# Two cross-attention layers on one core: the second batch's turned x and first context groups issued ahead of layer 1's value and output weights

## The chip, the cores and the metric

The kernel runs on 1 core of one Trainium2 chip. The metric is the device time of one execution in microseconds (us), the median of several runs.

## The reference

Eight batches (B = 8) with x of 512 x 256 and a context `ctx` of 1601 x 128, all float32, go through two cross-attention layers with the same context. Cut to what matters:

```python
# layer 0, for each batch: the softmax runs over the 512 rows of x (axis=1)
q = x @ Wq0 + bq0;  k = ctx @ Wk0 + bk0;  v = ctx @ Wv0 + bv0
w = softmax((q @ k.T) / 16, axis=query rows)
h = layernorm(w @ v + x) * gamma + beta
# layer 1: the softmax runs over the 1601 context rows
Q = h @ Wq1 + bq1;  K = ctx @ Wk1 + bk1;  V = ctx @ Wv1 + bv1
out = h + (softmax((Q @ K.T) / 16) @ V) @ Wo1 + bo1
```

## The kernel before

**Tiling.** The 1601 context rows are 13 tiles of at most 128 (`MT`), in 4 groups (`GROUPS`): three of four tiles (512 rows) and one of 65 rows. `ctxT` is the context turned, 128 x 1601; `xT` is x turned, two tiles of 128 x 512. The key and query weights are multiplied with each other once at the start (`make_w0`, `make_w1` item 0), so that the scores are taken straight from `ctxT` and a projected x. The value and output weights of layer 1 are multiplied with each other too, in `make_w1` item 1, which waits for `wv_loaded`.

**Order of the work.** Every engine follows an order that is written out by hand as a list of (step, batch, item): a head, a steady part repeated for four batches, and a tail. Engines meet only in semaphores. The steps that this text speaks of, with the line of each one's instruction:

- TensorE (PE). `project_q0(a)` (line 669) projects `xT` of batch a, and waits for `xT_loaded`. `project_bias0(a)` (676) turns a row sum `z0` into a row, `scores0(a, i)` (643 to 645, three matmuls) makes the layer-0 scores of context tile i, `weigh0(a, i)` (705) multiplies the context with the weights of tile i. `predict(0, h)` (643 to 645 again) makes the layer-0 result. Their order in the head around the change: scores0(0, 5), project_q0(1), scores0(0, 6), weigh0(0, 2), scores0(0, 7), weigh0(0, 3), (0, 4), (0, 5), scores0(0, 8), project_bias0(1).
- VectorE (DVE). `max0` (1086) takes scores out of PSUM and finds the least of each row of the negated ones; `recip0` (1093) is the reciprocal of a sum of exponentials; `q0_low` (1062) is one half of the split of the projected x; `sum_z0` (1076) makes `z0`; `ctxT_low` (1047) splits the turned context; `prepare_w1` item 0 (1228) adds `beta_row` and `bo_row`, item 2 (1241) makes `u1_gamma`, item 3 (1056) splits the value weights. In the order: max0(0, 5), ctxT_low(0, 3), recip0(0, 4), recip0(0, 5), q0_low(1), max0(0, 6), max0(0, 7), prepare_w1 item 0, recip0(0, 6), sum_z0(1), recip0(0, 7), max0(0, 8).
- ScalarE (ACT). `exp0` (919) and `norm0` (925) work on `p0`, the weights of one tile; `q0_high` (904), `ctx_split` (898) and `ctx_high` (890) round to fp32r; `copy_w1` (1017 to 1028) brings the prepared weights out of PSUM. In the order: exp0(0, 5), q0_high(1), norm0(0, 4), norm0(0, 5), ctx_split(0, 3), exp0(0, 6), ctx_split(1, 0), exp0(0, 7), ctx_split(1, 1), norm0(0, 6), norm0(0, 7), ctx_split(1, 2), ctx_high(1, 0), exp0(0, 8).
- GpSimd (POOL). `sum_weights(a, i)` (1284, 1287) adds `p0` of tile i to the running sum `wsum`, `weigh_u0(1)` (1318) multiplies x of batch 1 (the plain rows, `x_sb`, loaded by `load_x(1)`) with a row. In the order: sum_weights(0, 1), weigh_u0(1), sum_weights(0, 2), (0, 3), (0, 4), ctx_low(0, 3), sum_weights(0, 5), ...
- SyncE (SP) issues nearly all transfers, in the order of `pre0` and of the loop behind it. `load_xT(1)` waits for `qw0_ps` (project_q0(0) has read `xT_sb`), `load_ctxT(1, 0)` waits for the first `ctxT_low`; `load_ctx(1, 0)` waits for nothing.

**Rings.** `p0` has four slots for tiles 0 to 11 and a fifth for tile 12. `exp0(0, 6)` takes the slot of tile 2, and so waits for both its readers:

```python
if (held := before0(a, i)) is not None:
    back, last = held
    act.wait_ge(pv0_ps, MT * (a - back) + last + 1)
    act.wait_ge(wsum_done, summed(a - back, last))
```

and `weigh_u0(1)` begins with `pool.wait_ge(x_loaded[a % 2], 16 * (a // 2 + 1))`.

Of the kernel before, what the change touches and what calls it, by code (L numbers as in the profile page):

```python
# [300 lines left out]
def xattn_kernel(nc, x, xT, ctx, ctxT, wqT0, wkT0, wqT1, wkT1, wvT1, columns, wv0, bv0, gamma, beta, wo, bo, out):  # L301
    B, T, E = x.shape
    _, M, L = ctx.shape
    TB = T // P
    EC = E // P
    MT = -(-M // P)
    MPAD = M + M % 2
    GROUPS = -(-MT // TB)
# [35 lines left out]
    def rows(i):  # L344
        return min(P, M - i * P)

    def group(g):
        return range(TB * g, min(TB * g + TB, MT))

    def group_cols(g):  # L350
        return TB * g * P, min(M, TB * (g + 1) * P)
# [9 lines left out]
    with ExitStack() as stack:  # L361
# [196 lines left out]
        @blk.sync  # L558
        def _(sp):
            def load_x(c):  # L560
                if c >= 2:
                    sp.wait_ge(xbias_done, c - 1)
                sp.dma_start(x_sb[c % 2][:], x[bass.ds(c, 1)].rearrange("o (t p) e -> p (o t) e", p=P)
                             ).then_inc(x_loaded[c % 2], 16)

            def load_xT(c):

                if c >= 1:
                    sp.wait_ge(qw0_ps, c)
                sp.dma_start(xT_sb[:], xT[bass.ds(c, 1)].rearrange("o (c p) t -> p (o c) t", p=P)).then_inc(xT_loaded, 16)  # L570

            def load_ctxT(c, g):

                if c >= 1:
                    sp.wait_ge(ctxT_lo_done, GROUPS * (c - 1) + g + 1)
                lo, hi = group_cols(g)
                sp.dma_start(ctxT_sb[:, lo:hi], ctxT[bass.ds(c, 1), :, lo:hi].rearrange("o l m -> (o l) m")
                             ).then_inc(ctxT_loaded[g], 16)

            def load_ctx(c, g):  # L580

                if c >= 2:
                    sp.wait_ge(ctx_lo_done, GROUPS * (c - 2) + g + 1)
                    sp.wait_ge(pv0_ps, MT * (c - 2) + group(g)[-1] + 1)
                full = [i for i in group(g) if rows(i) == P]
                if full:
                    src = ctx[bass.ds(c, 1), full[0] * P:(full[-1] + 1) * P, :]
                    sp.dma_start(ctx_sb[c % 2][:, full[0]:full[-1] + 1, :], src.rearrange("o (i p) l -> p (o i) l", p=P)
                                 ).then_inc(ctx_loaded[c % 2][g], 16)
                else:  # L590
                    i = group(g)[0]
                    src = ctx[bass.ds(c, 1), i * P:M, :]
                    sp.dma_start(ctx_sb[c % 2][0:rows(i), i, :], src.rearrange("o p l -> (o p) l")).then_inc(ctx_loaded[c % 2][g], 16)

            def pre0():
                sp.dma_start(wqT[0], wqT0.rearrange("(h p) e -> p h e", p=P)).then_inc(w_loaded[0], 16)
                load_xT(0)
                load_ctxT(0, 0)
                load_x(0)
                load_ctx(0, 0)  # L600
                for g in range(1, GROUPS):
                    load_ctxT(0, g)
                    load_ctx(0, g)
                sp.dma_start(wqT[1], wqT1.rearrange("(h p) e -> p h e", p=P)).then_inc(w_loaded[1], 16)
                sp.dma_start(wkT[1], wkT1.rearrange("(h p) l -> p h l", p=P)).then_inc(w_loaded[1], 16)
                sp.dma_start(wv0_sb, wv0).then_inc(wv_loaded, 16)
                sp.dma_start(wvT, wvT1.rearrange("(h p) l -> p h l", p=P)).then_inc(wv_loaded, 16)
                sp.dma_start(wo_sb, wo.rearrange("(c p) d -> p c d", p=P)).then_inc(wv_loaded, 16)
                for row, v, landed in ((bv0_row[:], bv0, rows_loaded), (gamma_row[:], gamma, rows_loaded),
                                       (beta_row, beta, out_free[0]), (bo_row, bo, out_free[1])):  # L610
                    sp.dma_start(row, v.rearrange("(o e) -> o e", o=1).broadcast_to([P, E])).then_inc(landed, 16)
                load_x(1)

            def store(b):
                dst = out[bass.ds(b, 1)].rearrange("o (t p) e -> p (o t) e", p=P)
                for h in range(2):
                    sp.wait_ge(o_done, 2 * b + h + 1)
                    sp.dma_start(dst[:, 2 * h:2 * h + 2, :], y_res[:, 2 * h:2 * h + 2, :]
                                 ).then_inc(out_free[h], 16)

            pre0()
            for c in range(1, B + 3):
                if c < B:
                    load_xT(c)
                    for g in range(GROUPS):
                        load_ctx(c, g)
                        if g < GROUPS - 1:
                            load_ctxT(c, g)
                if c >= 3:
                    store(c - 3)  # L630
                if 2 <= c < B:
                    load_x(c)
                if c < B:
                    load_ctxT(c, GROUPS - 1)
            for h in range(2):
                sp.wait_ge(out_free[h], 16 * (B + 1))
# [3 lines left out]
        def _(pe):  # L640
# [22 lines left out]
            def project_q0(a, _):  # L663
                pe.wait_ge(xT_loaded, 16 * (a + 1))
                misc_free("project_q0", a)
                if a == 0:
                    pe.wait_ge(a0_done, 1)
                for c in range(EC):
                    mm = nc.tensor.matmul(ps_misc[:], a0_sb[:, c, :], xT_sb[:, c, :], start=(c == 0), stop=(c == EC - 1))  # L669
                mm.then_inc(qw0_ps, 1)  # L670

            def project_bias0(a, _):
                pe.wait_ge(z0_done, a + 1)
                misc_free("project_bias0", a)
                for t in range(TB):
                    mm = nc.tensor.transpose(ps_misc[:, t * P:(t + 1) * P], z0[:, t:t + 1].broadcast_to([P, P]), ident[:])
                mm.then_inc(cb_ps, 1)
# [698 lines left out]
```

## Time and profile before

| | us |
|---|---|
| median of 3 runs | 459.2 |
| lowest and highest run | 459.0 and 460.92 |
| the profiled execution, its own time | 460.37 |
| its span, first to last instruction | 458.4 |

In the profiled execution TensorE is busy for 430.9 us (94% of the span), VectorE 369.7 (81%), ScalarE 366.1 (80%), GpSimd 312.6 (68%). Some 2.0 us of the execution's time lie outside the span. The change touches the first 24 us of the kernel; times in the rows are counted from the start of the span.

### The profile page before, as it was taken

What the parts mean: (1) busy time and instruction counts of PE and PEld (TensorE: products, weight loads), DVE (VectorE), ACT (ScalarE), POOL (GpSimd) and SP (SyncE); (2) the same over time, 40 slices, a digit from 0 to 9 for tenths busy, and PEclk for the clock granted to TensorE, in tenths of its full rate; (3) what the DMA queues carried; (4) which work ended last, traced back from release to release, by engine and by line L of the source; (5) the groups of instructions that cost most, each with busy time, mean ns of one, the idle gap of its engine ahead of it and who ended that gap; (6) DMA issues with size and microseconds to landing.
All of it is one profiled execution on the core that took longest, in us unless ns stands there. A gap on an engine that the chain in (4) does not pass through costs nothing.

```text
span 458.4 us, 7304 instructions
## 1 busy us (share of the span) xinstructions
PE 430.9 (94%) x2192; PEld 340.9 (74%) x2192; DVE 369.7 (81%) x871; ACT 366.1 (80%) x776; POOL 312.6 (68%) x279
## 2 busy tenths in 40 slices
PE   7799799999999999999999999999999989897796
PEld 5555577788778877787788877787778876586696
DVE  3678887789778998799878998799788887586775
ACT  3877499989799878989799878988988788853473
POOL 1586489937996599847995599846995589813400
PEclk9999799999999999999999999999999999998999
DMA  8943012112132032302131032302200010000001
GB/s 273 287 140 93 19 54 72 48 46 74 48 98 65 1 117 73 94 0 76 45 115 48 1 117 74 93 1 68 54 1 1 0 46 2 1 1 23 24 1 46
DMA packets 31190, 28.00 MB, mean 61 GB/s; under 512 B 2856, under 2 KB 26032, under 8 KB 31152
## 3 DMA queue, kind: packets, MB, share of 16 engines
q1 hardware_dynamic: 30736, 27.41, 19.7%
q8 instruction: 17, 0.28, 0.3%
q10 hardware_dynamic: 416, 0.14, 0.1%
q14 instruction: 21, 0.17, 0.1%
HBM read 23.35 MB, written 4.19 MB: 60 GB/s over the span
## 4 chain that ended last, share of the span: by engine, by line
PE 73%; DVE 12%; ACT 6%; issue 3%; SPq 3%; DMA 2%; POOL 1%; DVEq 0%; ACTq 0%; POOLq 0%
PE ps_s L643 11%; PE ps_s L645 9%; PE ps_s L644 9%; PE ps_s L765 9%; PE ps_l L643 7%; PE ps_l L705 7%; PE ps_l L645 7%; PE ps_l L644 7%; ACT p L976 2%; DVE max L1170 2%; PE ps_l L669 2%; DMA xT_sb<-in_xT_dram 2%; DVE xhT_lo L1153 2%; DVE s_sb L1086 1%; DVE y_res L1213 1%
## 5 line engine op out<-in xcount | busy, mean ns | idle before, releaser
L1287 POOL TENSOR_TENSOR wsum<-wsum,p 128x512 f32<-128x512 f32 (+1 forms) x88 | 115.1, 1308 | 15.2 <-ACT p L925 7.5
L1294 POOL TENSOR_TENSOR p_lo<-p,p_hi 128x512 fp32r<-128x512 f32 (+1 forms) x49 | 63.8, 1303 | 44.9 <-ACT p_hi L933 44.7
L919 ACT ACTIVATE p<-s_sb,min 128x512 f32<-128x512 f32 (+1 forms) x104 | 75.0, 721 | 16.0 <-PE ps_l L705 9.5
L925 ACT ACTIVATE p<-p,r 128x512 f32<-128x512 f32 (+1 forms) x104 | 73.0, 720 | 7.0 <-DVE r L1093 6.9
L1086 DVE CUSTOM_DVE_ANT_0 s_sb<-ps_l,cb 128x512 f32<-128x512 f32 (+1 forms) x104 | 70.1, 686 | 10.2 <-PE ps_l L645 6.1
L1170 DVE TENSOR_REDUCE max<-ps_s 128x1 f32<-128x804 f32 x58 | 57.5, 993 | 16.4 <-PE ps_s L645 14.9
L1098 DVE TENSOR_TENSOR p1T_lo<-ps_s,p1T_hi 128x512 fp32r<-128x512 f32 (+1 forms) x91 | 59.8, 684 | 11.6 <-ACT p1T_hi L984 10.9
L984 ACT CAST p1T_hi<-ps_s 128x512 fp32r<-128x512 f32 (+1 forms) x91 | 51.2, 586 | 17.3 <-PE ps_s L765 9.8
L976 ACT ACTIVATE p<-ps_s,bias 128x1206 f32<-128x1206 f32 (+1 forms) x58 | 53.1, 920 | 3.8 <-DVE bias L1181 3.7
L705 PE MATMUL ps_l<-p,ctx_sb 128*128 128x512 f32 (+1 forms) x110 | 55.4, 596 | 0.0
L643 PE MATMUL ps_l<-qw_hi,ctxT_lo 128*128 128x512 f32 (+1 forms) x104 | 51.3, 493 | 1.2 <-DVE ctxT_lo L1047 0.8
L765 PEld LDWEIGHTS ps_s<-ident,p 128*128 128x128 f32 (+1 forms) x364 | 42.7, 140 | 10.4 <-issue 2.6
L765 PE MATMUL ps_s<-ident,p 128*128 128x128 f32 (+1 forms) x364 | 49.6, 273 | 0.4 <-ACT p L976 0.4
L1275 POOL TENSOR_TENSOR ctx_lo<-ctx_sb,ctx_hi 128x512 fp32r<-128x512 f32 (+1 forms) x32 | 34.4, 1079 | 16.9 <-ACT ctx_hi L898 16.9
L643 PE MATMUL ps_s<-ctxT_hi,qw_lo 128*128 128x402 f32 x116 | 42.1, 363 | 2.4 <-ACT p L976 1.6
L643 PE MATMUL ps_s<-p1T_hi,ctx_lo 128*128 128x512 f32 (+2 forms) x104 | 43.3, 416 | 0.6 <-DVE p1T_lo L1193 0.6
L644 PE MATMUL ps_l<-qw_lo,ctxT_hi 128*128 128x512 f32 (+1 forms) x104 | 41.5, 399 | 0.0
L645 PE MATMUL ps_l<-qw_hi,ctxT_hi 128*128 128x512 f32 (+1 forms) x104 | 41.5, 399 | 0.0
L645 PE MATMUL ps_s<-ctxT_hi,qw_hi 128*128 128x402 f32 x116 | 39.9, 344 | 0.0
L644 PE MATMUL ps_s<-ctxT_lo,qw_hi 128*128 128x402 f32 x116 | 39.8, 343 | 0.0
L644 PE MATMUL ps_s<-p1T_lo,ctx_hi 128*128 128x512 f32 (+2 forms) x104 | 39.7, 382 | 0.0
L645 PE MATMUL ps_s<-p1T_hi,ctx_hi 128*128 128x512 f32 (+2 forms) x104 | 39.5, 380 | 0.0
(161 smaller groups left out, 1039.7 us busy)
## 6 DMA issues: line engine op xcount, KB each, us to landing
ctxT_sb<-in_ctxT_dram SPq DMA_DIRECT2D x24, 256.0 KB, 2.7
ctx_sb<-in_ctx_dram SPq DMA_DIRECT2D x24, 256.0 KB, 3.2
xT_sb<-in_xT_dram SPq DMA_DIRECT2D x8, 512.0 KB, 3.8
x_sb<-in_x_dram SPq DMA_DIRECT2D x8, 512.0 KB, 4.1
out_dram<-y_res SPq DMA_DIRECT2D x16, 256.0 KB, 2.2
p<-in_wqT_dram SPq DMA_DIRECT2D x2, 256.0 KB, 4.0
ctxT_sb<-in_ctxT_dram SPq DMA_DIRECT2D x8, 32.5 KB, 1.8
ctx_sb<-in_ctx_dram SPq DMA_DIRECT2D x8, 32.5 KB
```

The source lines that it names most:

```text
L643: nc.tensor.matmul(ps, w_lo, m_hi, start=start, stop=False)
L644: nc.tensor.matmul(ps, w_hi, m_lo, start=False, stop=False)
L645: return nc.tensor.matmul(ps, w_hi, m_hi, start=False, stop=stop)
L705: mm = nc.tensor.matmul(ps_acc0[:], ctx_sb[a % 2][0:m, i, :], p0[0:m, ring0(i), :], start=first, stop=last)
L765: mm = nc.tensor.transpose(ps_turn[i % 3][0:m, t * P:(t + 1) * P], p1[:, t, i * P:i * P + m], ident[:])
L919: nc.scalar.activation(p0[0:m, ring0(i), :], s0_sb[0:m, (a + i) % 2, :], ACT.Exp, bias=min0[0:m, i:i + 1], scale=-1.0, accum_out=sum0[0:m, ...
L925: nc.scalar.activation(p0[0:m, ring0(i), :], p0[0:m, ring0(i), :], ACT.Copy, scale=r0[0:m, i:i + 1]).then_inc(norm0_done, 1)
L976: nc.scalar.activation(exps, scores, ACT.Exp, bias=bias1[:, t:t + 1], scale=1.0, accum_out=sum1[:, h, t:t + 1]).then_inc(exp1_done, 1)
L1086: nc.vector.tensor_tensor_reduce(out=s0_sb[0:m, (a + i) % 2, :], in0=ps_s0[0:m, (a + i) % 2, :], in1=cb[a % 2][0:m, :], scale=-SCALE, scal ...
L1170: nc.vector.tensor_reduce(max1[:, t, k:k + 1], s1_banks(b, t)[:, 2 * k:2 * k + 2, 0:CHUNK], AX_XY, ALU.max).then_inc(max1_done, 1)
L1287: nc.gpsimd.tensor_tensor(total, total, p0[0:m, ring0(i), :], ALU.add).then_inc(wsum_done, 1)
L1294: nc.gpsimd.tensor_tensor(p0_lo[0:m, h, :], p0[0:m, ring0(i), :], p0_hi[0:m, h, :].bitcast(F32), ALU.subtract).then_inc(p0_lo_done, 1)
```

## The change

In `pre0` of SyncE three transfers are issued right behind the query and key weights of layer 1: `load_xT(1)` (512 KB), `load_ctxT(1, 0)` (256 KB) and `load_ctx(1, 0)` (256 KB). The layer-0 value weights `wv0`, the layer-1 weights `wvT` and `wo`, four row vectors spread over the partitions (`bv0_row`, `gamma_row`, `beta_row`, `bo_row`) and `load_x(1)` follow them. The loop leaves the three out in its first turn. No other engine's program changes.

```diff
                 sp.dma_start(wkT[1], wkT1.rearrange("(h p) l -> p h l", p=P)).then_inc(w_loaded[1], 16)
+                load_xT(1)
+                load_ctxT(1, 0)
+                load_ctx(1, 0)
                 sp.dma_start(wv0_sb, wv0).then_inc(wv_loaded, 16)
                 sp.dma_start(wvT, wvT1.rearrange("(h p) l -> p h l", p=P)).then_inc(wv_loaded, 16)
                 sp.dma_start(wo_sb, wo.rearrange("(c p) d -> p c d", p=P)).then_inc(wv_loaded, 16)
...
             for c in range(1, B + 3):
+                if 1 < c < B:
+                    load_xT(c)
                 if c < B:
-                    load_xT(c)
                     for g in range(GROUPS):
-                        load_ctx(c, g)
-                        if g < GROUPS - 1:
-                            load_ctxT(c, g)
+                        if (c, g) != (1, 0):
+                            load_ctx(c, g)
+                            if g < GROUPS - 1:
+                                load_ctxT(c, g)
```

## Rows read from the trace of the kernel before

**Rows 1.** TensorE's timeline, 7 to 50 us: start, us, instructions, [idle before <-releaser].

```profile
7.86 1.96 PE L669 MATMUL ps_l<-xT_sb,a_sb 128*128 128x512 f32 x4
...
22.36 1.98 PE L669 MATMUL ps_l<-xT_sb,a_sb 128*128 128x512 f32 x4 [1.98 <-DMA xT_sb<-in_xT_dram]
...
30.55 0.65 PE L676 MATMUL ps_l<-ident,z 128*128 128x128 f32 x4 [0.68 <-DVE z L1076]
...
33.28 1.03 PE L855 MATMUL ps_s<-p 128*128 128x256 f32 x4
...
49.67 0.58 PE L643 MATMUL ps_l<-wv_hi,at_lo 128*128 128x256 f32 x1 [1.57 <-DVE xr L1126]
```

**Rows 2.** SyncE's timeline, 9 to 16 us: start, us to issue, transfer.

```profile
9.46 0.47 SPq L606 DMA_DIRECT2D p<-in_L_xattn_Wv_dram  x1
...
12.89 0.43 SPq L563 DMA_DIRECT2D x_sb<-in_x_dram  x1
13.37 0.51 SPq L570 DMA_DIRECT2D xT_sb<-in_xT_dram  x1
...
15.41 1.36 SPq L577 DMA_DIRECT2D ctxT_sb<-in_ctxT_dram  x1
```

**Rows 3.** The last three of these issues in the DMA view: size, us from issue to landing.

```profile
x_sb<-in_x_dram SPq DMA_DIRECT2D x1, 512.0 KB, 8.0
xT_sb<-in_xT_dram SPq DMA_DIRECT2D x1, 512.0 KB, 8.9
ctxT_sb<-in_ctxT_dram SPq DMA_DIRECT2D x1, 256.0 KB, 8.5
```

**Rows 4.** The chain that ended last, 40 to 50 us, in order of time.

```profile
40.93 0.24 PE ps_l L645
...
41.33 0.18 DVE s_sb L1086
```

**Rows 5.** GpSimd's timeline, 17 to 44 us.

```profile
20.97 2.34 POOL L1318 TENSOR_TENSOR xr<-x_sb,u_row 128x1024 f32<-128x1024 f32 x1 [2.13 <-DMA x_sb<-in_x_dram]
23.28 4.10 POOL L1287 TENSOR_TENSOR wsum<-wsum,p 128x512 f32<-128x512 f32 x3
...
36.78 6.95 POOL L1287 TENSOR_TENSOR wsum<-wsum,p 128x512 f32<-128x512 f32 x5 [2.64 <-ACT p L925]
```

**Rows 6.** ScalarE's timeline, 26 to 31 us.

```profile
26.50 0.72 ACT L919 ACTIVATE p<-s_sb,min 128x512 f32<-128x512 f32 x1
...
27.73 0.72 ACT L919 ACTIVATE p<-s_sb,min 128x512 f32<-128x512 f32 x1
...
29.41 0.72 ACT L925 ACTIVATE p<-p,r 128x512 f32<-128x512 f32 x1 [0.36 <-DVE r L1093]
30.60 0.72 ACT L925 ACTIVATE p<-p,r 128x512 f32<-128x512 f32 x1 [0.46 <-DVE r L1093]
```

**Rows 7.** VectorE's timeline, 21 to 43 us.

```profile
21.18 2.22 DVE L1047 TENSOR_TENSOR ctxT_lo<-ctxT_sb,ctxT_hi 128x65 fp32r<-128x65 f32 x1
...
29.30 1.20 DVE L1076 TENSOR_REDUCE z<-xr 128x4 f32<-128x1024 f32 x1
...
39.63 1.56 DVE L1241 SCALAR_TENSOR_TENSOR u_gamma<-p,gamma_row 128x256 f32<-128x256 f32 x1
41.33 0.69 DVE L1086 CUSTOM_DVE_ANT_0 s_sb<-ps_l,cb 128x512 f32<-128x512 f32 x1
...
41.95 0.65 DVE L1056 TENSOR_TENSOR wv_lo<-p,wv_hi 128x256 fp32r<-128x256 f32 x1
```

**Rows 8.** Busy us by stretch: PE, PEld, DVE, ACT, POOL, PEclk, DMA share, GB/s.

```profile
15.00:18.00 3.00, 3.00 (x13) 2.05 (x13) 1.51 (x5) 2.69 (x6) 0.74 (x2) 1.00 0.60 155
18.00:24.00 6.00, 4.02 (x14) 2.16 (x12) 4.12 (x11) 3.87 (x11) 3.87 (x3) 1.00 1.06 344
...
30.60:41.40 10.80, 10.80 (x48) 7.66 (x49) 7.85 (x23) 10.80 (x24) 7.59 (x7) 1.00 0.24 74
49.60:55.80 6.20, 6.13 (x18) 4.79 (x18) 5.93 (x20) 2.74 (x6) 3.08 (x4) 0.51 0.00 0
```

## The prediction

> **What bounds the kernel now.** I read TensorE's timeline first. It stands still for 1.98 us before project_q0(1), until the turned x of batch 1 has landed [rows 1], while ahead of that transfer on SyncE's queue lie weights and rows that nobody wants for another 5 to 10 us. That is what the change is about, and 1.98 us is the most that its direct effect can give. Behind it, in 30.6 to 41.4 us, TensorE and ScalarE are both busy without a gap [rows 8]. So both must get earlier for the end to get earlier. From 41.33 us the chain of waits runs on VectorE, started by the score matmul that ends at 41.17 [rows 4]. VectorE hands over at 49.67 us, when TensorE has waited 1.57 us for it at predict(0, 1) [rows 1]. After that TensorE is nearly always busy, and a shift of this point passes to the end one for one. The question is thus when VectorE's work of 41.33 us starts afterwards.
>
> **Part 1: the moved transfers.** Landings follow from issue and duration [rows 2, 3]: x(1) at 12.89 + 8.0 = 20.9, xT(1) at 13.37 + 8.9 = 22.3, ctxT(1, 0) at 15.41 + 8.5 = 23.9 us. GpSimd's start at 20.97 and TensorE's at 22.36 agree [rows 1, 5]. They land in the order of issue, and each waits some 8 us: the queue is backed up, so a place in it is what counts. xT(1), ctx(1, 0) and ctxT(1, 0), 1 MB, take from 20.93 to 23.9, 2.97 us.
> Afterwards xT(1) has ahead of it neither the 512 KB of value and output weights, nor four spread rows, nor x(1). That is 1.5 MB less, at the 344 GB/s of 18 to 24 us [rows 8] 4.6 us: it lands by 17.7 us, rather sooner, since the spread rows were slower than that. TensorE, which comes at 22.36 - 1.98 = 20.38 us, doesn't wait: minus 1.98 us there.
> The added wait: SyncE comes to load_xT(1) at 9.46 us [rows 2] and must wait until project_q0(0) has read the old xT, 7.86 + 1.96 = 9.8 us [rows 1]: some 0.4 us, with all later issues queued behind it. The wait for the first ctxT_low is over by then. The queue's backlog of several us covers the 0.4; if it were empty, the transfers behind would be 0.4 late. The three extra issues, 0.5 us each, lie under the same cover. The weights for make_w1 item 1 and the spread rows land ahead of x(1), so before 23.9 us; the first are wanted at 33.28 [rows 1], and prepare_w1 item 0, which wants rows, isn't reached before 25.1. The context groups behind the moved ones have the same bytes ahead as before.
>
> **Part 2: what becomes late.** x(1) now has 1 MB more ahead: 20.93 + 2.97 = 23.9 us. Bounds: at the 344 GB/s of 18 to 24 us [rows 8] 1 MB takes 3.05 us; if the three lie in a stretch like 15 to 18 us, 155 GB/s, 6.8 us. That slow stretch falls on the spread rows, which pass whole both times, so I take the near value, 2.97. Nothing of it is a gain: at best x(1) stays at 20.93.
> GpSimd already waits 2.13 us for x(1) [rows 5], and its order puts weigh_u0(1) before sum_weights(0, 2). It starts at 23.95, ends 2.31 later at 26.26, and the sum of tile 2 takes 1.27: 27.53 us. ScalarE's exp0(0, 6) takes over tile 2's slot and must wait for that sum. Now the sum is ready at 23.28 + 1.37 = 24.6 and exp0(0, 6) starts at 26.50 without waiting for it [rows 6]; afterwards it starts at 27.6, 1.1 us later than before, though its scores are 2 us earlier. The next, exp0(0, 7), follows the sum of tile 3, at 28.97 against 27.73: plus 1.24.
> ScalarE makes up its two idle pieces, 0.36 and 0.46 us [rows 6], because VectorE's reciprocals are no longer what it waits for. With one of the usual steps of 0.63 between, norm0(0, 6) comes at 30.3 and norm0(0, 7) at 30.9, against 30.60: plus 0.3 us. From there to 41.4 us ScalarE has no gap [rows 8], so exp0(0, 8), the reciprocals, norm0(0, 8) and copy_w1 items 1 to 3 are all 0.3 late.
>
> **Part 3: TensorE between.** It does scores0(0, 6) to (0, 8) and four weighings some 2 us earlier, and stands at project_bias0(1) from 27.6. sum_z0(1) is behind recip0(0, 6) on VectorE, which follows exp0(0, 6): 27.6 + 0.82 + 0.1 = 28.5, plus 1.2 for the reduction [rows 7]: 29.75 us against 30.50. So of 1.98 us TensorE keeps 0.75. It loses 0.4 of this again at weigh0(0, 8), whose norm0 is ScalarE's, and makes the score matmul of 41.17 us end at about 40.8.
>
> **Part 4: VectorE at 41.33.** It doesn't start there at 40.97, for u1_gamma (1241) comes before. That step needs copy_w1 item 1 (plus 0.3), and it took 1.56 us, from 39.63 to 41.19, though it is 128 x 256 [rows 7]. ctxT_low of 65 columns took 2.22 us, and ended as GpSimd's weigh_u0 did [rows 5, 7]: such a step waits until GpSimd's running instruction is over. GpSimd's five sums start with norm0(0, 8), 0.3 late, so the sum that lets u1_gamma go ends 0.3 late too: 41.5 us. VectorE goes on at 41.55 to 41.6 instead of 41.33, and the value split (1056), which also took 0.65 us between GpSimd's sums, is released 0.3 later. The sum is **plus 0.3 us** at 49.67 and at the end. Profiled execution: 460.37 + 0.3 = 460.7; it lies 1.2 above the median of the runs, so on the median's scale 459.2 + 0.3 = **459.5 us**.
> The least that this can be: if GpSimd's timing lets VectorE through and only TensorE decides, minus 0.36 (458.8). The most: weigh_u0 and the sums now run without pause until 36 us, and ctxT_low(1, 0) and the split of a1_gamma lie under them; each can wait up to 1.3 us. They have about 0.6 us of room before norm0(0, 9) and exp0(0, 11) wait for them. One more such hit gives plus 1.0 (460.2).
>
> **Two rules weighed.** The row shows a 65-column ctxT_low of 2.22 us beside GpSimd's 2.34 us multiplication [rows 5, 7]. The Trainium skill, "SBUF — State Buffer", section "Who interferes with whom", says that a VectorE instruction with two SBUF inputs and a GpSimd one that reads SBUF exclude each other for the whole instruction, and that PSUM-fed or one-input steps are free. The trace agrees; by this rule weigh_u0 from 23.95 lies on prepare_w1 item 0 instead of on ctxT_low(0, 3), and without the rule part 4 would come out at minus 0.3.
> The rows give 2.97 us for the moved 1 MB. The Trainium skill, "DMA: Bandwidth & Descriptors", section "Where 436 GB/s comes from", puts the fabric's ceiling at 435 GB/s, and HBM's at about 358. At 435 it would be an estimated 2.4 us and the sum minus 0.3; at 358 it would be 2.9. The trace's 344 GB/s stands near the second.
>
> **Rivals.** (a) *The full gain.* If exp0(0, 6) weren't held by x(1), ScalarE, TensorE and VectorE would all move by the 1.98 us: 457.2. ScalarE's shift is x(1)'s landing minus 23.6 us, so this needs x(1) by 21.6. For it: the slow stretch of 155 GB/s [rows 8] might be due to the order of the queue and vanish, and then x(1) lands up to 2 us sooner. Against it: the DMA engines are full in 18 to 24 us. Chance 0.18, cases between 457.0 and 458.6.
> (b) *x(1) later still* (the other side). It lands behind weights, rows and 1 MB; if the slow stretch gets longer, ScalarE, and with it VectorE, is late by landing minus 23.6. x(1) at 25.6 gives plus 2.0, 461.2; it is slower by over 0.5%, 2.3 us, from 25.9 us on. For it: GpSimd has no slack at all here. Against it: the same bytes. Chance 0.14.
> (c) *The clock.* TensorE's idle time moves from before project_q0(1) to before project_bias0(1), 2.1 us. In 49.6 to 55.8 the granted clock is 0.51, the level of 1.2 GHz, after a stretch with long waits, and TensorE, with 6.13 us busy there, would have needed about half [rows 8]. A second such stretch costs up to 3 us (462.5), and the loss of the existing one gives up to 3 back (456.5). The gap now, as long, brought no fall. Chance 0.05 each.
> (d) *It doesn't do what it says*: SyncE's wait at 9.46 lets the queue run dry and xT(1) is late as before. That needs a wait of several us; it is 0.4. Chance under 0.01.
>
> **The numbers.** The forecast, 458.7 to 460.3, has 0.58. Half a per cent, 2.3 us, is about what a measurement of this kernel can tell from no change. The range of 8 in 10 takes in most of (a) and (b): 457.2 to 461.3. Faster by over 0.5% (below 456.9): the best of (a) and the clock's gain, 0.09. Slower by over 0.5% (above 461.5): the worst of (b) and the clock's loss, 0.10. Within: 0.81.
>
> **What would show it.** TensorE's line 669 at about 20.3 with no wait for DMA; GpSimd's line 1318 at 23.9 after 5 us of waiting; ScalarE's line 919 at 27.6 released by GpSimd's 1287; TensorE idle some 2 us before line 676, at 29.8; VectorE's 1086 at 41.5; predict(0, 1) at about 50.0. If line 1318 starts before 23, I am wrong on the queue; if it starts at 23.9 and line 919 doesn't wait, on the ring.

## The result, and the profile after

The changed kernel takes **461.37 us** (median of 20 runs, 460.13 to 463.25) against 459.11 (20 runs, 456.27 to 461.21): ratio **1.0052**, 95% interval 1.0036 to 1.0067. It is slower by about 2.3 us, where 459.5 was forecast. The profiled execution took 461.36 us, with a span of 459.3.

VectorE's row sum of line 1104 (1109 afterwards) runs once per batch and marks how far the kernel has got. VectorE's timeline of batch 0, before and then after:

```profile
46.39 0.68 DVE L1104 TENSOR_REDUCE rowsum<-ps_l 128x4 f32<-128x512 f32 x1
```

```profile
49.46 0.68 DVE L1109 TENSOR_REDUCE rowsum<-ps_l 128x4 f32<-128x512 f32 x1
```

In batch 0 the row sum comes 3.07 us later. In batch 1 the distance is 2.45 us, and it stays at 2.4 up to the last batch (406.15 and 408.55). So all of the loss is there by 49 us, and 0.6 of it is made up by batch 1. That the two spans differ by only 0.9 us comes from the execution of before: from its last row sum to its end it took 52.3 us, and every other profiled execution of this study 50.7 to 50.8. Only its TensorE was at the lower clock for a while at 415 us. The view of stretches, before and then after (columns as in [rows 8]):

```profile
415.00:420.00 5.00, 3.60 (x18) 3.07 (x17) 2.90 (x10) 2.56 (x5) 2.05 (x2) 0.75 0.00 0
```

```profile
415.00:420.00 5.00, 3.60 (x20) 2.75 (x19) 4.34 (x15) 2.12 (x5) 1.39 (x2) 1.00 0.00 0
```

Such stretches differ from execution to execution, and the record has the mean granted clock of each. Over the 90 executions of the kernel before in the rounds of the experiments it goes from 0.985, with a median time of 461.3 us, to 0.996, with 457.3. The 20 of the changed kernel lie between 0.985 and 0.993. Where both had 0.989 (22 and 9 executions), the medians are 459.5 and 461.4, so some 1.9 of the 2.3 us are there at an equal mean clock.

The queue first. SyncE's timeline of the changed kernel, and behind it the landings of bv0, bo and x(1):

```profile
9.09 0.47 SPq L605 DMA_DIRECT2D p<-in_wkT_dram  x1
10.62 0.37 SPq L570 DMA_DIRECT2D xT_sb<-in_xT_dram  x1
...
13.55 0.47 SPq L614 DMA_DIRECT2D bv_row<-in_L_xattn_bv_dram  x1
...
15.01 0.44 SPq L614 DMA_DIRECT2D p<-in_L_xattn_bo_dram  x1
15.49 0.43 SPq L563 DMA_DIRECT2D x_sb<-in_x_dram  x1
```

```profile
bv_row<-in_L_xattn_bv_dram SPq DMA_DIRECT2D x1, 128.0 KB, 5.0
p<-in_L_xattn_bo_dram SPq DMA_DIRECT2D x1, 128.0 KB, 8.3
x_sb<-in_x_dram SPq DMA_DIRECT2D x1, 512.0 KB, 9.3
```

SyncE stood for 1.0 us before xT(1), not 0.4, because project_q0(0) ended later in this execution. The spread rows land from 18.6 us (bv0) to 23.3 (bo), x(1) at 24.8. In this stretch the transfers ran at 128, 76, 154 and 206 GB/s in the four us from 18 to 22. That is the slow stretch of [rows 8], a us longer than before. GpSimd, ScalarE and TensorE of the changed kernel, each from its timeline:

```profile
24.89 2.35 POOL L1323 TENSOR_TENSOR xr<-x_sb,u_row 128x1024 f32<-128x1024 f32 x1 [5.87 <-DMA x_sb<-in_x_dram]
27.20 4.27 POOL L1292 TENSOR_TENSOR wsum<-wsum,p 128x512 f32<-128x512 f32 x3
```

```profile
28.77 0.72 ACT L924 ACTIVATE p<-s_sb,min 128x512 f32<-128x512 f32 x1 [4.34 <-POOL wsum L1292]
...
38.82 1.34 ACT L930 ACTIVATE p<-p,r 128x512 f32<-128x512 f32 x2 [0.44 <-DVE r L1098]
41.06 0.72 ACT L924 ACTIVATE p<-s_sb,min 128x512 f32<-128x512 f32 x1 [0.90 <-DVE min L1091]
```

```profile
20.41 1.88 PE L674 MATMUL ps_l<-xT_sb,a_sb 128*128 128x512 f32 x4
...
30.97 1.12 PE L681 MATMUL ps_l<-ident,z 128*128 128x128 f32 x4 [3.16 <-DVE z L1081]
...
52.73 0.58 PE L648 MATMUL ps_l<-wv_hi,at_lo 128*128 128x256 f32 x1 [1.13 <-DVE xr L1131]
```

The reader sees the forecast chain step by step, only longer. TensorE comes to xT(1) at 20.41 without a wait (1.98 us before, [rows 1]). GpSimd waits 5.87 us for x(1) and starts at 24.89 (20.97, [rows 5]). exp0(0, 6) is released by GpSimd's sum and starts at 28.77 (26.50, [rows 6]). TensorE stands 3.16 us before project_bias0(1). Then two things come that the sum didn't have. TensorE's clock falls to its lower level, 1.2 GHz, at 30.0 us, about 2.2 us into this wait, and stays there until about 36.8:

```profile
30.00:31.00 1.00, 0.03 (x1) 0.03 (x1) 0.91 (x1) 0.91 (x4) 0.86 (x2) 0.51 0.06 16
31.00:32.00 1.00, 1.00 (x5) 1.00 (x6) 0.85 (x3) 1.00 (x2) 1.00 (x3) 0.50 0.00 0
```

And on VectorE several steps that have their inputs in SBUF have grown. Its timeline, before and then after:

```profile
33.86 0.83 DVE L1047 TENSOR_TENSOR ctxT_lo<-ctxT_sb,ctxT_hi 128x512 fp32r<-128x512 f32 x1
34.62 0.47 DVE L1233 TENSOR_SCALAR p<-p,cols 128x128 f32<-128x128 f32 x2
...
35.79 0.22 DVE L1093 RECIPROCAL r<-sum 128x1 f32<-128x1 f32 x2
35.92 0.67 DVE L1047 TENSOR_TENSOR ctxT_lo<-ctxT_sb,ctxT_hi 128x512 fp32r<-128x512 f32 x1
```

```profile
35.44 1.08 DVE L1052 TENSOR_TENSOR ctxT_lo<-ctxT_sb,ctxT_hi 128x512 fp32r<-128x512 f32 x1
36.44 1.49 DVE L1238 TENSOR_SCALAR p<-p,cols 128x128 f32<-128x128 f32 x2
...
38.63 0.21 DVE L1098 RECIPROCAL r<-sum 128x1 f32<-128x1 f32 x2
38.77 1.65 DVE L1052 TENSOR_TENSOR ctxT_lo<-ctxT_sb,ctxT_hi 128x512 fp32r<-128x512 f32 x1
```

The two scalings of a1_gamma went from 0.47 us to 1.49, ctxT_low(1, 0) in front of them from 0.83 to 1.08 and the next one behind them from 0.67 to 1.65. I call *VectorE's stretch* the time from the start of ctxT_low(1, 0) to the start of recip0(0, 9) and (0, 10): 33.86 to 35.79, 1.93 us, before; 35.44 to 38.63, 3.19 us, after. The experiments take the lateness of x(1), the clock and this stretch apart.

### The profile page after: what moved, and what is told of

The parts are those of the page before. It is cut to its first block, busy times and chain, and to the rows that moved or that the text cites. A ratio compares the mean times of both kernels' runs of the same rounds, so it can differ in the third digit from the quotient of the medians.

```text
span 459.3 us, 7304 instructions
## 1 busy us (share of the span) xinstructions
PE 432.0 (94%) x2192; PEld 342.2 (74%) x2192; DVE 369.3 (80%) x871; ACT 366.3 (80%) x776; POOL 313.9 (68%) x279
## 4 chain that ended last, share of the span: by engine, by line
PE 70%; DVE 11%; ACT 7%; issue 6%; POOL 5%; DVEq 0%; ACTq 0%; POOLq 0%
PE ps_s L648 10%; PE ps_s L650 9%; PE ps_s L649 9%; PE ps_s L770 8%; PE ps_l L710 7%; PE ps_l L648 7%; PE ps_l L650 6%; PE ps_l L649 6%; ACT p L981 2%; DVE max L1175 2%; PE ps_l L674 2%; DVE xhT_lo L1158 2%; DVE s_sb L1091 1%; DVE y_res L1218 1%; POOL wsum L1289 1%
```

## The experiments

All were timed in five rounds beside the kernel before, and the ratio is to its executions in the same rounds (medians 458.81 to 458.97 us; 459.11 beside the changed kernel). Differences from before are taken within the rounds. "x(1)" is the start of weigh_u0(1) in the profiled execution, "row sum" the start of VectorE's row sum of batch 0, "ScalarE waits" its wait for VectorE's reciprocal before norm0(0, 9), and the clock is the granted one in 28 to 40 us.

| kernel | x(1) | VectorE's stretch | ScalarE waits | clock | row sum | median us | ratio, 95% interval |
|---|---|---|---|---|---|---|---|
| before | 20.97 | 1.93 | none | 1.00 | 46.39 | 459.11 | |
| changed | 24.89 | 3.19 | 0.44 | 0.50 for 6.8 us | 49.46 | 461.37 | 1.0052 (1.0036 to 1.0067) |
| e1_fill | 24.53 | 4.39 | 1.73 | 1.00 | 49.18 | 460.79 | 1.0040 (1.0018 to 1.0062) |
| e5_fill_quiet | 24.84 | 2.36 | none | 1.00 | 48.14 | 460.07 | 1.0015 (0.9995 to 1.0036) |
| e10_after_quiet | 24.83 | 2.35 | none | 1.00 | 48.09 | 460.53 | 1.0041 (1.0016 to 1.0066) |
| e4_x_late | 23.67 | 4.38 | 1.73 | 1.00 | 48.34 | 461.75 | 1.0074 (1.0046 to 1.0101) |
| e11_late_again | 23.83 | 4.38 | 1.73 | 1.00 | 48.48 | 461.12 | 1.0062 (1.0040 to 1.0084) |
| e9_late_quiet | 25.05 | 2.36 | none | 1.00 | 48.34 | 459.17 | 1.0018 (0.9993 to 1.0044) |
| e7_xT_only | 22.48 | 4.40 | 1.73 | 1.00 | 47.33 | 460.91 | 1.0038 (1.0009 to 1.0068) |
| e12_xT_again | 23.34 | 4.39 | 1.73 | 1.00 | 47.99 | 461.05 | 1.0057 (1.0030 to 1.0084) |
| e3_sums_first | 24.36 | 4.71 | 2.06 | 1.00 | 46.14 | 458.27 | 0.9994 (0.9977 to 1.0011) |
| e6_rows_last | 20.56 | 2.73 | none | 1.00 | 44.90 | 457.17 | 0.9962 (0.9939 to 0.9984) |
| e2_x_first | 19.71 | 2.53 | none | 1.00 | 44.33 | 456.03 | 0.9938 (0.9914 to 0.9961) |
| e8_x_first_quiet | 19.20 | 1.78 | none | 1.00 | 43.58 | 455.99 | 0.9925 (0.9896 to 0.9955) |

**e1_fill: TensorE kept busy in its gap.** The changed kernel, and:

```diff
-    ("project_bias0", 1, 0), ("scores0", 0, 9), ...
+    ("fill", 0, 13), ("project_bias0", 1, 0), ("scores0", 0, 9), ...
+            def fill(_, n):
+                for _ in range(n):
+                    nc.tensor.matmul(s1_bank(1)[:, 0:P], ident[:], ident[:], start=True, stop=True)
```

> The changed kernel with 13 matmuls of ident by ident (128 columns, into an unused PSUM bank) put before project_bias0(1) on TensorE, where it stood idle for 3.16 us; nothing else. Theory (the late x makes the gap, and the gap brings the clock down to 1.2 GHz from 31 to 37 us, which costs most of the loss): the gap is filled, the granted clock stays at 1.00 from 28 to 40 us, project_bias0(1) still starts at 31.0, and the time comes down by 1.0 to 1.8 us against the changed kernel, to 459.6 to 460.4, ratio to before 1.001 to 1.003. Rival (the clock stretch costs nothing of its own, since ScalarE and GpSimd are as late from x alone): the same as the changed kernel, ratio 1.005.

The gap is filled and the clock stays at 1.00, but only 0.6 us come back in the median, and the intervals of the two kernels overlap. The loss stays, and shows itself elsewhere: ScalarE, with TensorE now earlier, waits 1.73 us for a reciprocal. VectorE's timeline of this kernel:

```profile
34.95 1.25 DVE L1057 TENSOR_TENSOR ctxT_lo<-ctxT_sb,ctxT_hi 128x512 fp32r<-128x512 f32 x1
36.12 1.50 DVE L1243 TENSOR_SCALAR p<-p,cols 128x128 f32<-128x128 f32 x2
37.66 0.30 DVE L1246 CAST a1g_hi<-p 128x256 fp32r<-128x256 f32 x1
37.99 1.42 DVE L1248 TENSOR_TENSOR a1g_lo<-p,a1g_hi 128x256 fp32r<-128x256 f32 x1
39.34 0.21 DVE L1103 RECIPROCAL r<-sum 128x1 f32<-128x1 f32 x2
```

The clock theory falls as the main cause; 0.6 us is under the 1.0 to 1.8 that it asked for.

**e2_x_first: x(1) right behind xT(1).** The changed kernel with one line moved:

```diff
                 load_xT(1)
+                load_x(1)
                 load_ctxT(1, 0)
...
-                load_x(1)
```

> The changed kernel with load_x(1) issued right behind load_xT(1), so ahead of the two context transfers, the weights and the rows. Theory (all the loss comes from x(1) landing 4 us later): x(1) lands by 18 us, GpSimd's line 1318 starts at 18.9 without a wait, exp0(0, 6) doesn't wait, TensorE waits neither at project_q0(1) nor much at project_bias0(1); the full 1.5 to 2 us are gained against before: 457.2 to 457.7, ratio 0.995 to 0.997. Rival (the spread rows, now landing at about 25 us, hold prepare_w1 item 0 on VectorE, or the weights come late): ratio 0.999 or above, with a DMA named before line 1228.

456.03 us, 2.9 below before: more than expected, and more than the 1.98 us of TensorE's wait. At the row sum it is 2.1 us early, the wait and little more; where the rest comes from isn't shown. GpSimd starts weigh_u0(1) at 19.71 with no wait for a transfer, and TensorE has no wait between 18 and 45 us. Everything that the change moved is still moved; so the harm lay in what fell behind it, and that is x(1) (the weights and rows are still behind the moved transfers and do no harm).

**e3_sums_first: GpSimd's order.** The changed kernel, with weigh_u0(1) behind two sums:

```diff
-    ("sum_weights", 0, 1), ("weigh_u0", 1, 0), ("sum_weights", 0, 2), ("sum_weights", 0, 3),
+    ("sum_weights", 0, 1), ("sum_weights", 0, 2), ("sum_weights", 0, 3), ("weigh_u0", 1, 0),
```

> The changed kernel with GpSimd's weigh_u0(1) moved behind sum_weights(0, 2) and (0, 3); SyncE's order stays as changed. Theory (x(1)'s lateness reaches ScalarE only through the order on GpSimd): exp0(0, 6) starts at 24.4 and not 28.8, though x(1) still lands at 24.8; sum_z0 ends at 28.9, TensorE's gap before project_bias0(1) is about 1.3 us, no fall of the clock before 45 us; time 457.5 to 458.5, ratio 0.996 to 0.999. Rival (sum_z0 itself, which needs x, is what holds TensorE): gap still near 3 us and the clock falls, ratio 1.004 or above.

458.27 us: within its window of 457.5 to 458.5, though the ratio, 0.9994, is just above the 0.996 to 0.999 given with it. x(1) lands as late as ever, but exp0(0, 6) starts at 24.65 and TensorE's gap shrinks to 0.25 us. The ring of p0 is thus the way from x(1) to ScalarE, as part 2 had it. That it isn't as good as e2_x_first goes with a VectorE stretch of 4.71 us and a 2.06 us wait of ScalarE.

**e4_x_late and e11_late_again: x(1) late, nothing else.** The kernel before:

```diff
                     for g in range(GROUPS):
                         load_ctx(c, g)
                         if g < GROUPS - 1:
                             load_ctxT(c, g)
+                        if (c, g) == (1, 0):
+                            load_x(1)
```

> The kernel before with one transfer moved the other way: load_x(1) is issued behind xT(1), ctx(1, 0) and ctxT(1, 0) instead of ahead of them; weights and rows stay in front. x(1) should land at 23.9 us, the very value of the prediction, xT(1) at 20.9. Theory (prediction's sum, part 2 to 4, with the clock as a threshold that a gap of 2.2 us doesn't reach): exp0(0, 6) at 27.6, no fall of the clock before 45 us, time 459.4, ratio 1.000 to 1.002. Rival (any late x brings the clock down): gap over 2 us, granted clock 0.50 in 31 to 36 us, ratio 1.004 to 1.006.

> The late x alone once more, word for word the same kernel, for a second profile: the first profile was its fastest run, 460.05, and the runs spread from 460 to 465. Theory (the spread is TensorE's clock falling at the gap before project_bias0(1) in some executions and not in others): this profile, if its time is 461.5 or more, shows a granted clock of 0.50 somewhere in 28 to 46 us. Rival: a slow profile shows 1.00 there and the difference lies elsewhere. Median 461 to 462.5.

This tests the sum at its own value, since x(1) comes at 23.67. exp0(0, 6) starts at 27.58, where part 2 gave 27.6 (for an x(1) 0.28 us later than here), and TensorE's gap is 1.76 us at a clock of 1.00. And yet it is slower by 0.74%, where the sum says 0.3 us. Neither theory was right: no clock falls before 46 us, and the time isn't 459.4. ScalarE's and TensorE's timelines show where the sum fails:

```profile
27.58 0.72 ACT L920 ACTIVATE p<-s_sb,min 128x512 f32<-128x512 f32 x1 [2.95 <-POOL wsum L1288]
...
38.68 1.33 ACT L926 ACTIVATE p<-p,r 128x512 f32<-128x512 f32 x2 [1.73 <-DVE r L1094]
```

```profile
37.09 1.10 PE L706 MATMUL ps_l<-p,ctx_sb 128*128 128x512 f32 x2 [0.44 <-ACT p L926]
39.45 1.13 PE L706 MATMUL ps_l<-p,ctx_sb 128*128 128x512 f32 x2 [1.26 <-ACT p L926]
```

The second profile (460.16 us) shows the same rows, so it doesn't tell what the slower executions have: both profiled ones were the fastest of their kernel, 1 to 1.7 us under the median. The granted clocks on record go with it in part: the seven executions of the pair with a mean of 0.989 or less took 461.6 to 464.9 us, the twelve others 460.1 to 462.4. Where in the kernel the slower ones had the lower clock no trace shows, so e11_late_again's theory stays open.

**e5_fill_quiet, e9_late_quiet, e10_after_quiet: GpSimd's pause put back.** On e1_fill, on e4_x_late and on the changed kernel the same edit:

```diff
-    ("sum_weights", 0, 7), ("ctx_low", 1, 0), ("sum_weights", 0, 8), ...
-    ("sum_weights", 0, 12), ("ctx_low", 1, 1), ...
+    ("sum_weights", 0, 7), ("sum_weights", 0, 8), ...
+    ("sum_weights", 0, 12), ("ctx_low", 1, 0), ("ctx_low", 1, 1), ...
```

> The changed kernel with the 13 filler matmuls, and GpSimd's ctx_low(1, 0) moved from behind sum_weights(0, 7) to behind sum_weights(0, 12); x(1) still lands at 24.5 us. Theory (x(1)'s lateness removes GpSimd's pause at 34 to 37 us, so that VectorE's ctxT_low(1, 0) and prepare_w1 item 1 are blocked between max0(0, 10) and recip0(0, 10): 4.39 us there against 1.93 before, and ScalarE waits 1.73 us for the reciprocal): the pause comes back, that stretch shrinks to about 2.5 us, the 1.73 us wait goes, and the time comes down by 1.2 to 1.7 us against the filler alone, to 459.1 to 459.6, ratio 1.000 to 1.002. Rival (ScalarE's own lateness of 1.2 us at exp0(0, 8) decides and the blocking lies beside it): not more than 0.5 us better, ratio 1.003 to 1.004.

> The kernel before with load_x(1) issued behind xT(1), ctx(1, 0) and ctxT(1, 0), so x(1) lands at 23.7, and GpSimd's ctx_low(1, 0) moved from behind sum_weights(0, 7) to behind sum_weights(0, 12). Theory (the blocking of VectorE under GpSimd's unbroken work, which made ScalarE wait 1.73 us in the first run of the late x, is what my sum left out; the rest of the sum holds): no 1.73 us wait, rowsum on VectorE (46.39 before) within 0.5 us of its old place, time 459.0 to 460.0, ratio 1.000 to 1.003, at least 1.2 us better than the late x alone. Rival (ScalarE's lateness through the ring is larger than my sum said): ratio 1.005 and above.

> The changed kernel with GpSimd's ctx_low(1, 0) moved behind sum_weights(0, 12), no filler. Theory (in the changed kernel TensorE at 1.2 GHz from 31 to 37 us is as late as VectorE's blocked steps, so that either cause alone hides the other): nearly nothing is gained without the filler, 460.5 to 461.3, ratio 1.004 to 1.005. Rival (the two add up): 0.7 to 1.2 us better than the changed kernel, about 460.3, ratio 1.003.

GpSimd's ctx_low(1, 0) lies on VectorE's stretch when x(1) is late. GpSimd's timeline of e4_x_late, then that of e9_late_quiet:

```profile
30.67 4.13 POOL L1288 TENSOR_TENSOR wsum<-wsum,p 128x512 f32<-128x512 f32 x3
34.77 1.73 POOL L1276 TENSOR_TENSOR ctx_lo<-ctx_sb,ctx_hi 128x512 fp32r<-128x512 f32 x1
37.03 1.26 POOL L1288 TENSOR_TENSOR wsum<-wsum,p 128x512 f32<-128x512 f32 x1 [0.53 <-ACT p L926]
```

```profile
32.03 4.15 POOL L1288 TENSOR_TENSOR wsum<-wsum,p 128x512 f32<-128x512 f32 x3
38.38 7.25 POOL L1288 TENSOR_TENSOR wsum<-wsum,p 128x512 f32<-128x512 f32 x5 [2.21 <-ACT p L926]
```

VectorE's timeline of e9_late_quiet, to be held against that of e1_fill above:

```profile
35.46 1.26 DVE L1048 TENSOR_TENSOR ctxT_lo<-ctxT_sb,ctxT_hi 128x512 fp32r<-128x512 f32 x1
36.65 0.47 DVE L1234 TENSOR_SCALAR p<-p,cols 128x128 f32<-128x128 f32 x2
...
37.48 0.43 DVE L1239 TENSOR_TENSOR a1g_lo<-p,a1g_hi 128x256 fp32r<-128x256 f32 x1
37.82 0.22 DVE L1094 RECIPROCAL r<-sum 128x1 f32<-128x1 f32 x2
```

In e4_x_late ctx_low lies on the scalings, from 35.28 us on. They end late, and so the split of a1_gamma starts at 37.14, just behind GpSimd's next sum at 37.03, and is held as well. With ctx_low gone that sum starts at 38.38, when the stretch is over. In all three the stretch shrinks to 2.35 or 2.36 us and ScalarE's wait goes. The scalings are back to 0.47 us, the split to 0.43. The medians fall by 0.7 us (e1_fill to e5), 0.8 (changed to e10) and 2.0 to 2.6 (e4 and e11 to e9). Each pair's intervals overlap or nearly meet, but all go the same way. e9_late_quiet is at plus 0.4 us by the medians (0.8 by the ratio), though x(1) came as late as 25.05. Its expectation missed in one place: the row sum was at 48.34, 1.95 late and not within 0.5, and 1.3 of that was made up by batch 1. e5_fill_quiet missed its time: 460.07 and not 459.1 to 459.6, 0.7 us better than e1_fill where its theory asked for 1.2 to 1.7 and its rival for 0.5 at most. e10_after_quiet doesn't decide between its theory and its rival: 460.53 lies at the edge of the one's 460.5 to 461.3, and 0.8 us better in the other's 0.7 to 1.2.

The row sums decide more than the medians. VectorE's timeline of e10_after_quiet, to be held against 49.46 in the changed kernel:

```profile
48.09 0.68 DVE L1109 TENSOR_REDUCE rowsum<-ps_l 128x4 f32<-128x512 f32 x1
```

The row sum starts 24.57 us behind weigh_u0(1) in the changed kernel, and 24.65 to 24.67 behind it in e1_fill, e4_x_late, e11_late_again and e12_xT_again. In the three kernels with the pause it starts 23.26 to 23.30 us behind it. So the blocked stretch costs 1.3 to 1.4 us there, with x(1) at 23.3 or at 24.9, and apart from that the row sum of these eight executions moves with x(1) one for one. On top of a blocked stretch TensorE's slow clock adds nothing that can be seen at this point: 24.57, with 6.8 us of it, is the least of the five. Whether it costs something where the stretch is short no profile shows, for that of e10_after_quiet has a clock of 1.00.

**e6_rows_last: x(1) ahead of the spread rows.** The changed kernel, with `load_x(1)` between `wo` and the rows:

```diff
                 sp.dma_start(wo_sb, wo.rearrange("(c p) d -> p c d", p=P)).then_inc(wv_loaded, 16)
+                load_x(1)
                 for row, v, landed in ((bv0_row[:], bv0, rows_loaded), ...
...
-                load_x(1)
```

> The changed kernel with load_x(1) issued ahead of the four spread rows, still behind xT(1), the two context transfers, wv0, wvT and wo. Theory (the spread rows are the slow part of the queue, 4 to 5 us for 512 KB, and what makes the moved 1 MB harmful is that x(1) lies behind both): x(1) lands at about 20 us, exp0(0, 6) doesn't wait, the rows land by 25.5, about when VectorE wants them; 456.0 to 457.0, ratio 0.993 to 0.996. Rival (the rows, now last, hold VectorE at line 1228): 458 or more, ratio 0.998 or above.

x(1) is used at 20.56, 4.3 us sooner than in the changed kernel, with the moved 1 MB and the weights still in front. 457.17 us is just above the window of 456.0 to 457.0, and 0.8 us below the rival's 458. Passing the four rows (512 KB) brought x(1) 4.3 us; the moved 1 MB had cost it 3.9.

**e7_xT_only and e12_xT_again: only xT(1) moved.**

```diff
+                load_xT(1)
                 sp.dma_start(wv0_sb, wv0).then_inc(wv_loaded, 16)
...
-                    load_xT(c)
+                    if c > 1:
+                        load_xT(c)
```

> The kernel before with load_xT(1) alone moved ahead of the value and output weights; ctx(1, 0) and ctxT(1, 0) stay in the loop. Theory (dose: each us of x(1) past 22 us costs about one): x(1) lands at 22.5 to 23.0, exp0(0, 6) starts at 26.2 to 26.7, about where it was, and the blocking on VectorE is in between; 458.5 to 460.0, ratio 0.999 to 1.002, better than the changed kernel by 1.5 to 2.5 us. Rival (the SyncE wait or another consequence of moving xT(1) does the harm, not the bytes ahead of x(1)): as bad as the changed kernel, ratio 1.005.

> xT(1) alone ahead of the weights once more, the same kernel, for a second profile: the first was 458.7 and the runs spread from 457.7 to 462.5. Theory (the same spread by the clock, here by the stretch at 40 to 46 us, where the first profile had 0.72): a profile of 461 or more shows more time at 0.50 in 28 to 60 us than the first. Rival: x(1) lands at another time in it (22.5 us in the first), by 1 us or more. Median 460 to 461.5.

The dose theory missed its number: with half of the bytes moved and exp0(0, 6) at 26.20, 0.3 us *earlier* than before, the kernel is still 1.0038 of before, and 1.0057 in the second comparison. The stretch is 4.4 us and ScalarE waits its 1.73 in both. So exp0(0, 6) needn't be late. x(1) is, by 1.5 us, and that is enough to take GpSimd's pause away: its sums and ctx_low(1, 0) run without one from 29.32 to 35.14 us and the next sum from 35.67, over most of VectorE's stretch of 32.74 to 37.14. x(1) came 0.9 us later in the second profile, and exp0(0, 6) started at 27.23; in the first, the clock was at 0.72 in the stretch of 40 to 46 us, in the second at 1.00.

**e8_x_first_quiet: both at once.** e2_x_first with the edit of e5.

> The kernel with load_x(1) right behind load_xT(1), and GpSimd's ctx_low(1, 0) moved behind sum_weights(0, 12). Theory (VectorE's stretch between max0(0, 10) and recip0(0, 10) is 2.5 us there, 0.6 over the unblocked one, and nothing waits for it): no more than 0.3 us better than without the move, 455.7 to 456.2, ratio 0.993 to 0.994. Rival (GpSimd's five sums end later or the blocking counts here too): a difference of over 0.7 us either way.

455.99 us, no different in the median from e2_x_first, with a stretch of 1.78 us. Nothing waits for it there. This and e2_x_first are the fastest kernels of the study, 0.6 to 0.75% under before. So the edit by itself gains nothing in the time where x(1) is early.

## Why the prediction was wrong

- **Part 1, the moved transfers** held: xT(1) lands before TensorE wants it and the 1.98 us go. SyncE's wait was 1.0 us and not 0.4, and nothing shows that it cost anything.
- **Part 2, x(1)** held in its mechanism (e3_sums_first shows the ring, e2_x_first the landing), but its first term was mis-sized. I put x(1) 2.97 us later, at 23.9; it came 3.92 later, at 24.89. I took the spread rows to cost the same in both orders; from bv0's landing to bo's it was 4.1 us before and 4.8 afterwards. Nor does an order fix the landing: x(1) was used at 23.67, 23.83 and 25.05 in three executions with one and the same SyncE order. At 24.89 the rule "ScalarE's shift is landing minus 23.6" gives plus 1.3 in place of 0.3; measured at exp0(0, 8), 33.67 against 32.26, 1.4. This term alone is thus about 1 us short.
- **Part 3** held: sum_z0(1) came at 29.70, where 28.5 was forecast, about the us by which x(1) came later than forecast; the gap is 3.16 instead of 2.1.
- **Part 4 is the step that failed.** It names the blocking of ctxT_low(1, 0) and the split of a1_gamma under GpSimd's unbroken work, with 0.6 us of room, and then enters it as the upper bound of the sum and not as a term. I asked only how many two-input steps might be hit, and left out the two scalings. e4_x_late has x(1) where I had it, and the wait is there: 4.38 us instead of 1.93, and 1.73 us of ScalarE. Of the 2.45 us of growth the two named steps have 0.42 and 1.00, and the scalings, which I had at nothing, 1.03. Putting the pause back takes the wait away in three kernels, and 1.3 to 1.4 us at the row sum in each. In the medians that is 2.0 to 2.6 us for the late pair and 0.7 to 0.8 for the other two; why these differ isn't shown.
- **Rival (b)**, x(1) later still, had the sign, but asked for a landing at 25.9 for 0.5%; 24.9 did it, with the blocked stretch on top. **Rival (c)**, the clock, came about in the profiled execution (chance given 0.05) and isn't what makes the loss: e1_fill, without it, is at 1.0040. Nor does the length of the gap alone decide it: in the changed kernel the clock fell about 2.2 us into it, and in e10_after_quiet TensorE stood for 2.89 us and the clock stayed at 1.00. Whether the clock has 0.6 us of the 2.3 can't be told from the intervals; the row sum shows none of it from this stretch. **Rival (a)**, the full gain, wasn't this change, but is what e2_x_first gets: x(1) by 21.6 was its condition, and 19.7 gives minus 2.9 us.
- On the two rules: the Trainium skill, "SBUF — State Buffer", section "Who interferes with whom", also says that a tensor_scalar on VectorE in a mode that uses two ports contends with GpSimd, and that a tensor_reduce doesn't. The part of the page that the prediction told, that one-input steps are free, holds there only outside such a mode. The runs agree: the pair of scalings takes 0.47 us beside a resting GpSimd and 1.50 beside a working one, and the reduction of sum_z0 took 1.19 to 1.22 us in every kernel. Had I gone by that sentence, the scalings would have been in the sum.

The whole: of the 3.07 us at the first row sum, 1.4 are gone in e10_after_quiet, whose profile has neither the blocked stretch nor the slow clock, and the two kernels that differ by the stretch alone at a clock of 1.00 (e1_fill and e5_fill_quiet) show as much for it. The 1.7 that are left go with the lateness of x(1) through the ring; 0.9 of these are the landing that the sum had too early and 0.3 what it had. The last 0.5 isn't placed. In the medians the split is wider: of the 2.3 us, 0.7 to 2.6 go with the stretch, 0.4 (e9_late_quiet) to 1.7 (e10_after_quiet) stay when it is short, and the clock has up to 0.6. The parts overlap, and no finer split is shown.

## What to carry to other kernels

On a queue that is backed up, a transfer moved forward is another moved back: look first for the waits that already exist for those behind it, and move them together. GpSimd's 2.13 us wait for x(1) stood in the profile of before, and 512 KB more in the right place turned plus 2.3 into minus 2.9 us. An engine's pause can be what lets another engine work: before filling GpSimd's idle time, count every VectorE step with SBUF inputs that lies on it, not only the costly ones.

## What the runs showed of the hardware

- Four transfers that spread one row of 1 KB over 128 partitions, 512 KB in all, go with the slowest stretch of the queue. In the changed kernel bv0 landed at 18.6 and bo at 23.3 us, and in 18 to 22 us the transfers ran at 76 to 206 GB/s, beside 320 to 380 in the us before 17 and behind 23; in single us of other executions the rate fell to 28 (e9_late_quiet) and 67 GB/s (e12_xT_again). Whether the spreading itself is slow wasn't tested apart.
- Two scalings of 128 x 128 took 0.47 us or 1.49 to 1.51, by what GpSimd did. So did a split of 128 x 256 (0.43 in e9_late_quiet, 1.42 in e1_fill) and a cast of it (0.30 in e1_fill, 1.24 in e3_sums_first).
- TensorE idle for 3.16 us in the changed kernel went with 6.8 us at 1.2 GHz, begun about 2.2 us into the idle time; idle for 2.89 us (e10_after_quiet) with none, in the stretch of 31 to 34 us:

```profile
31.00:34.00 3.00, 3.00 (x14) 2.24 (x15) 1.52 (x5) 3.00 (x6) 2.86 (x4) 1.00 0.00 0
```
